# Attention edge loops of a graph network: exponentials and rescaled sum in PSUM, weighted values in a tile of their own

## What is computed

```python
def _L1_gnn_ref(node_features, edge_index, edge_relations, ...):      # 4 heads of 64
    mod_k = K[src] + 0.2 * rel_w[edge_relations][:, None, :]
    scores = jnp.einsum('ehd,ehd->eh', Q[dst], mod_k) / D ** 0.5
    ex = jnp.exp(scores - segment_max(scores, dst)[dst])
    w = ex / segment_sum(ex, dst)[dst]
    agg = segment_sum(w[:, :, None] * V[src], dst)
...
def _L2_gnn_ref(x, edge_attr, ...):                                   # 8 heads of 32
    key_j = k[src] + (edge_attr @ We + be).reshape(-1, H, C)
    alpha = softmax((q[dst] * key_j).sum(-1) / math.sqrt(C), axis=0)
    out = segment_sum(v[src] * alpha[:, :, None], dst)
```

## Time and profile before

| | us |
|---|---|
| median of three runs | 4558.12 (4556.85 to 4558.42) |
| the profiled execution, its time | 4554.94 |
| its span from first to last instruction | 4553.1 |
| layer 1, first to last L1751 | 799.7 (1832.3 to 2632.0) |
| layer 2, first to last L1751 | 844.2 (2894.8 to 3739.0) |

### The profile page before, as it was taken

The page is one execution under the profiler, slowest core; times in us unless marked ns, Lnnn a source line. Parts: engine busy times, 40 slices in busy tenths (PEclk is TensorE's granted clock), DMA queues, the critical chain, the costliest instruction groups (busy, mean ns, idle before and its releaser), DMA issues. The chain is left out here.

```text
span 4553.1 us, 52726 instructions
## 1 busy us (share of the span) xinstructions
PE 2757.1 (61%) x11454; PEld 1449.6 (32%) x11454; DVE 3258.7 (72%) x7572; ACT 720.5 (16%) x2122; POOL 3148.8 (69%) x2929
## 2 busy tenths in 40 slices
PE   4245678888885997666566757687877763000006
PEld 4145322222222885222222334344443432000004
DVE  7498358888885333788889966588888886666664
ACT  0011100000000332333323321111111112000003
POOL 0577667767664776777777757677777764777772
PEclk8555799999998998788878778778788876555558
DMA  3235346666664332655555632456666652444441
GB/s 155 41 104 157 80 139 177 177 173 172 176 173 126 57 63 58 165 160 161 160 159 163 177 67 67 134 166 168 167 167 165 169 136 60 108 108 108 108 107 41
DMA packets 408930, 594.52 MB, mean 131 GB/s; under 512 B 267146, under 2 KB 273430, under 8 KB 407806
## 3 DMA queue, kind: packets, MB, share of 16 engines
q0 software_dynamic: 185552, 519.27, 41.5%
q1 hardware_dynamic: 223278, 74.01, 6.9%
HBM read 532.97 MB, written 59.26 MB: 130 GB/s over the span
## 5 line engine op out<-in xcount | busy, mean ns | idle before, releaser
L1690 PE MATMUL edge_psX<-state,ident 128*128 128x512 f32 x720 | 480.5, 804 | 217.9 <-DMA state<-tab,edge_feat 134.3
L1106 POOL DMA_INDIRECT edge_ring<-tab,edge_rec x480 | 469.8, 979 | 146.2 <-issue 135.6
L2016 POOL DMA_INDIRECT state<-tab,edge_rec x480 | 453.8, 945 | 155.0 <-issue 145.9
L1685 PE MATMUL edge_psX<-edge_w_edge,edge_featT 64*128 64x256 f32 x1920 | 446.2, 454 | 119.6 <-DVE edge_prod L1752 117.0
L1615 POOL DMA_INDIRECT state<-tab,edge_rec x360 | 419.7, 1166 | 130.0 <-issue 108.8
L1615 POOL DMA_INDIRECT state<-tab,edge_feat x360 | 393.8, 1094 | 109.7 <-issue 100.8
L1135 PE MATMUL edge_psX<-state,ident 128*128 x720 | 380.4, 638 | 140.0 <-DVE edge_ring L1163 140.0
L1685 PEld LDWEIGHTS edge_psX<-edge_w_edge,edge_featT 64*128 64x128 f32 x1920 | 300.3, 220 | 412.6 <-issue 353.1
L2189 PE MATMUL gate_psA<-ident,gate_w_nat 128*128 128x128 f32 x8 | 2.0, 428 | 631.4 <-DMA gate_w_nat<-in_L_gnn_W_ih 631.4
L1163 DVE TENSOR_TENSOR edge_ring<-edge_psX,edge_ring 128x1024 f32<-128x1024 f32 x240 | 293.8, 1224 | 73.8 <-PE edge_psX L1142 43.8
L781 POOL DMA_INDIRECT sorted_d<-update_row_out,update_row_idx x200 | 237.7, 1189 | 91.8 <-issue 60.0
(11 more groups left out here) (447 smaller groups left out, 6513.4 us busy)
## 6 DMA issues: line engine op xcount, KB each, us to landing
sorted_d<-state SPq DMA_DIRECT2D x7, 2380.0 KB
state<-src_rows SPq DMA_DIRECT2D x25, 562.5 KB
state<-low_rows SPq DMA_DIRECT2D x25, 562.5 KB
state<-tab,edge_rec POOLq DMA_INDIRECT x840, 3.0
edge_ring<-tab,edge_rec POOLq DMA_INDIRECT x600, 3.7
update_row_out<-in_edge_attr SPq DMA_DIRECT2D x40, 156.2 KB
edge_rec<-rec_d SPq DMA_DIRECT2D x364, 8.0 KB, 2.9
state<-tab,edge_feat POOLq DMA_INDIRECT x360
```

What stands on the lines that cost most here:

```text
L1106: pool.indirect_dma_start(out=ring[:, k, s, :], out_offset=None, in_=S["tab0"][:, :], in_offset=bass.IndirectOffsetOnAxis(ap=rec[:, k, R_S ...
L1685: pe.matmul(psX[k % 2][:, s % 2, s // 2, :], featT[lo:lo + ED, k % 4, s // PAIR, :], w_edge[lo:lo + ED, :], start=(s < 2), stop=False, ski ...
L1690: last = pe.matmul(psX[k % 2][:, a, :, :], S["ident"][:, :], ring[k % RING].rearrange("p (c a) f -> p a c f", a=2)[:, a, :, 0:D], start=Fa ...
L2016: pool.indirect_dma_start(out=ring[:, k, s, :], out_offset=None, in_=S["tab3"][:, :], in_offset=bass.IndirectOffsetOnAxis(ap=rec[:, k, R_S ...
```

## The change

The tile `wgt`, two buffers in SBUF, into which ACT writes the exponentials, goes. In its place is `w`, one buffer in a PSUM bank of its own (`psW`). A second bank (`psS`) holds `so_far`, 256 numbers in each partition. The products of values and weights go to a tile `terms` in SBUF instead of back into the ring. The decayed `acc` is written to `so_far`, not in place; the first of the two remaining rows of `terms` is added to it in PSUM, and the last sum, of `so_far` and the second row, is written to `acc`. The post of s_done stands behind the halving instead of at the end of the step. The number of DVE instructions and of counted results in a step is the same.

```diff
-        wgt = ph.sb("wgt", [P, 2, ROWS, heads])
+        terms = ph.sb("terms", [P, QE, D])
...
+        psW, psS = (ph.ps(n, [P, 512]) for n in ("psW", "psS"))
+        w = psW[:, 0:ROWS * heads].rearrange("p (r h) -> p r h", h=heads)
+        so_far = psS[:, 0:D]
...
-                        act.activation(wgt[:, k % 2, :, :], cat[:, k % 2, :, :], ACT.Exp).then_inc(s_exp, 1)
+                        act.activation(w, cat[:, k % 2, :, :], ACT.Exp).then_inc(s_exp, 1)
...
+                def weigh(at):
+                    vals = ring[at][:, :, D:D2].rearrange("p s (h d) -> p s h d", h=heads)
+                    return dve.tensor_tensor(terms[:, :, :].rearrange("p s (h d) -> p s h d", h=heads), vals,
+                                             bc(w[:, 0:QE, :], 3, [P, QE, heads, hd]), ALU.mult)
+
+                def halve():
+                    return dve.tensor_tensor(terms[:, 0:2, :], terms[:, 0:2, :], terms[:, 2:4, :], ALU.add)
+
+                def decay(acc):
+                    return dve.tensor_tensor(so_far.rearrange("p (h d) -> p h d", h=heads), acc.rearrange("p (h d) -> p h d", h=heads),
+                                             bc(w[:, QE, :], 2, [P, heads, hd]), ALU.mult)
+
+                def add_half(to, i):
+                    return dve.tensor_tensor(to, so_far, terms[:, i, :], ALU.add)
...
                         hold(dve, s_exp, t * AQ + (k + 1))
                         step.put(dve.tensor_tensor(l, l, w[:, QE, :], ALU.mult))
-                        weighted = step.put(dve.tensor_tensor(vals, vals, bc(w[:, 0:QE, :], 3, [P, QE, heads, hd]), ALU.mult))
+                        weighted = step.put(weigh(at))
                         dve.wait_ge(s_xr, t * AQ + (k + 3))
                         scored = step.put(dve.tensor_reduce(score[:, 0:QE, :].rearrange("p s h -> p (s h)"),
                                                             prod[:, :, :].rearrange("p s (h d) -> p (s h) d", d=hd), AX.X, ALU.add))
                         b_next = block_of(k + 1, t) if k < AQ - 1 else None
                         step.put(dve.tensor_reduce(tot[:, :], w[:, 0:QE, :].rearrange("p r h -> p h r"), AX.X, ALU.add))
                         step.until(weighted)
-                        halved = step.put(dve.tensor_tensor(v[:, 0:2, :], v[:, 0:2, :], v[:, 2:4, :], ALU.add))
+                        halved = step.put(halve())
+                        dve.nop().then_inc(s_done[at], 1)
                         step.until(scored)
                         masked = step.put(dve.tensor_tensor(score[:, 0:QE, :], score[:, 0:QE, :], bc(mask, 2, [P, QE, heads]), ALU.add))
-                        step.put(dve.tensor_tensor(acc_h, acc_h, bc(w[:, QE, :], 2, [P, heads, hd]), ALU.mult))
+                        decayed = step.put(decay(acc))
                         step.until(masked)
                         dve.nop(nofuse=True)
                         highest = step.put(dve.tensor_reduce(m, score.rearrange("p r h -> p h r"), AX.X, ALU.max))
-                        step.until(halved)
-                        summed = step.put(dve.tensor_tensor(v[:, 0, :], v[:, 0, :], v[:, 1, :], ALU.add))
+                        step.until(decayed)
+                        summed = step.put(add_half(so_far, 0))
                         step.until(highest)
                         dve.tensor_tensor(score, score, bc(m, 1, [P, ROWS, heads]), ALU.subtract).then_inc(s_cat, 1)
                         step.put(dve.tensor_tensor(l, l, tot[:, :], ALU.add))
                         step.until(summed)
-                        step(dve.tensor_tensor(acc, acc, v[:, 0, :], ALU.add))
-                        dve.nop().then_inc(s_done[at], 1)
+                        step(add_half(acc, 1))
                         b_prev, b = b, b_next
```

More of the change, by code:

```diff
@@ L1715, in last_values @@
+                    step.put(decay(acc))
                     step(dve.tensor_reduce(tot[:, :], w[:, 0:QE, :].rearrange("p r h -> p h r"), AX.X, ALU.add))
-                    step(dve.tensor_tensor(v[:, 0:2, :], v[:, 0:2, :], v[:, 2:4, :], ALU.add))
-                    dve.tensor_tensor(acc_h, acc_h, bc(w[:, QE, :], 2, [P, heads, hd]), ALU.mult)
                     dve.tensor_tensor(l, l, tot[:, :], ALU.add)
-                    step(dve.tensor_tensor(v[:, 0, :], v[:, 0, :], v[:, 1, :], ALU.add))
```

14 lines of the change are left out of this document (5 added, 9 removed).

## The result

The changed kernel takes 4429.39 us (median of 4 runs, 4426.94 to 4430.56), the kernel before, measured beside it, 4557.49 us (4555.25 to 4558.42). The ratio is 0.9717, with an interval of 0.9706 to 0.9729: 128 us less. The forecast was 4450, with a range of 4420 to 4508. The profiled executions stand at 4430.56 and 4554.94 us, 124.4 us apart.

A forecast was written before the change was run, and what follows sets the result against it. The prediction took POOL, which issues the gathers, to bound the kernel, with DVE next. Savings of 39 us in layer 1 and 69 in layer 2 took the profiled 4554.9 to 4446.9, 4450 us as a median, range 4420 to 4508.

The forecast's parts named there:

- POOL as the bound and its reason: Both layers: POOL never waits; DVE instructions with two SBUF inputs hold its gathers and scatters, losing 104 and 100 us.
- a mean below 0.98 us: Sign of being right: L1615's gathers in both layers at a median of 946 ns and a mean under 0.98 us.
- 1.2 us a turn for the halving: POOL's remaining loss at gathers that start inside the halving, which keeps two SBUF inputs: 1.2 us a turn.
- The price of PSUM: DVE's step: the first sum's wait, the post and PSUM access together add 0.05 us a step, 6 us a layer.
- the rival with 0.07 an instruction: DVE's three 256-wide instructions each take 0.07 us more from PSUM: 4500 us; all six instructions, 4543; chance 0.09.
- the one with a product at half rate: Rival: DVE's product reads repeated PSUM weights at half rate, 1.07 us more each: +245 us, 4695; chance 0.04.
- The 512-wide row: Profile row used to price PSUM on DVE: 695 ns with 512 numbers, against 0.71 us with both inputs in SBUF.
- The post of s_done: DVE's step: moving the post out of the 0.27 us between steps gives perhaps 0.02 us back.
- The stall that goes with it: Layer 1: DVE's 5.01 us wait behind ACT's record wait moves 2 us earlier each turn, gone after the first.
- the case "it stayed": Layer 1: if the stall behind the record stayed, DVE would need 55.3 us a turn.
- Meshing in layer 2: Layer 2: POOL's 51.0 and DVE's 50.9 us turns don't mesh perfectly, adding 0.6 us a turn, 9 us.
- The sum: Layer 1 760.5 us (-39), layer 2 775.4 us (-69), together -108: 4446.9 us profiled, 4450 as a median.

The follow-up runs named there:

- weights_only_again: The changed kernel with the sums back in SBUF and the weights still in PSUM, a repeat run: 4431.2 us, 0.9728 of the kernel before.
- long runs: Follow-up runs in three of four groups, where every kernel took longer, the kernel of before by 17% (5332 to 5351 us); compared only among themselves.

## Why the prediction was right, point by point

**POOL as the bound and its reason: right.** 1.88 us became 0.95 us beside the product, and taking the weights back out of PSUM brought the long gathers back. The forecast of a mean below 0.98 us (0.975 and 0.973) holds, and so does that of 1.2 us a turn for the halving (some 13 us in 14.9 turns of layer 1 are 0.9, some 16 in layer 2 are 1.1). By the Trainium skill, "SBUF — State Buffer", section "Who interferes with whom", a `tensor_tensor` with both inputs in SBUF takes only a reading interface of the port that DVE shares with GpSimd, so that the making of descriptors is not touched (the page calls that inferred). The traces of both kernels and of the experiments disagree with that inference, with 1.88 against 0.95 us and means of 1.12 against 0.975. Which part of a gather is held they don't tell: it also reads its indices from `edge_rec` in SBUF.

**The price of PSUM: right, a little low in one place.** Of the +0.05 us a step, 0.06 was for the first sum's wait for the decay, -0.02 for the post, and next to nothing for PSUM. Measured, the product has -5 ns, the decay +8, the first sum +22, the last +1 or 2: +0.03 in durations. Neither the rival with 0.07 an instruction nor the one with a product at half rate has anything left. The 512-wide row was the better guide than the 256-wide one with another form. The wait was put too high: no run shows the 0.08 us that I took for the way of a semaphore. The first sum starts 0.03 us behind the decay's end (2105.76 after 2105.73), where it was 0.02, so its dependence cost some 0.01 and not 0.06. This and the longer sums together are the 0.03 us that weights_only_again saves. The weights in PSUM took 0.05 us off the step, which I hadn't foreseen.

**The post of s_done: mis-sized.** "Perhaps 0.02 back" was 0.11 to 0.12 us in each step. The 0.27 us of idle time before L1751 stood in the earlier trace rows, and I took it for the way of a semaphore from DVE's last sum to its next instruction. More than a third of it was the post, a `nop` that waited for that sum. Beside that the rest is small: with nothing in PSUM the step is 5.92 us, with the weights there 5.87, with the sums too 5.90. Instead of +0.05 a step there were -0.14. In floors: 731.5 us in layer 1 where 752.5 was forecast, and in layer 2, with a turn of 49.75 us, 738 where 761.4 was: 44 us below in all.

**The stall that goes with it: wrong.** "It lies earlier by 2 us more in each turn and no longer holds DVE after the first turn." It stayed in all of turns 1 to 10, at 1.6 us of DVE's time each, and 11 us in the first. The step that failed is the thought that a POOL with less work than DVE gains on it turn by turn. POOL can gain only as long as nothing holds it, and the same record that ACT waits for holds POOL too. The chain from the last scatter over SP's three loads to the record is closed by POOL itself, and 50.9 us of circle are more than DVE's 49.3. I had added up POOL's issues (47.4 us and about 1 for the halving) and left out its own wait at the turn's head, 2.2 us, which comes with the way over SP. The price of the case "it stayed" was wrong as well: not 55.3 but 50.9 us a turn, since the circle had shortened with the gathers. Layer 1 lay 28 us above its floor, where 8 were forecast. DVE's share in layer 1 (89%, "over 95%" forecast) and ACT's waits (86.9 us, "nearly gone") are the same error. POOL did sit idle for records there, as forecast, but not for want of a free slot: the wait is at the turn's head, behind the scatter. That sign came true for another reason.

**Meshing in layer 2: somewhat low.** 24 us above the floor against 5 + 9. The mean turn is 51.3 us over a floor of 49.75; POOL is full (717.7 of 720 us), with a turn of 49.8 us and 1.1 for the halving, and DVE has 91%, not 95. Since DVE turned out quicker, POOL, and not both alike, is what is left of the bound there. That is read from the busy times, not tested.

**The sum.** Errors of -44 (step) and +30 (20 in layer 1's stall, 10 in layer 2) gave a forecast that is 14 us too high in the two layers, and 4450 against 4429. The other 6 to 7 us are 2 us gained outside these spans and 4 to 5 from the step to the median: the forecast added 3.2 us to the profiled time, which lay 1.2 above the median. The total was close in part because two errors of layer 1 cancelled: -21 and +20. Its -39 against -40 looks better than it was.

## What to carry to other kernels

Where GpSimd's indirect DMAs are the bound, look for DVE instructions with two inputs in SBUF beside them, and give the longest one an input in PSUM: with the 20 or 40 weights a partition there, stalls of 147 to 164 us fell to about 30, and the sums added nothing to the gain that can be measured. A post on a semaphore at the end of a dependent step waits for that step and delays the next one; put it behind the last read of what it frees, where other work hides it. And when an engine comes off the bound, follow each wait around its whole circle before writing it off: a stall whose far end hangs on that same engine doesn't run away from it.

## What the runs showed of the hardware that was not expected

- A post behind the last instruction of a step cost 0.11 to 0.12 us (a step of 6.01 to 6.02 us with it, 5.90 without); DVE sits idle for 0.26 us ahead of the next step instead of 0.15.
- PSUM as input, or as input and output, of the 256-wide instructions costs 1 to 22 ns. The Trainium skill, "VectorE: DVE Perf Modes", section on the TRN2 errata, gives VectorE a fixed part of 58 cycles from SBUF and 120 from PSUM; the rows don't show such a difference (410 and 432 ns for the first sum, 1219 and 1214 for the product).
- In long runs the kernel of before lost 17%, with DVE waiting at "issue" for 1 to 2 us in front of its instructions, and the loss was not the same for all. With the weights in PSUM the kernels were 1.6 to 1.9% slower than the code of before beside them, while with the sums alone it was 0.2 to 0.6% and with neither nothing. Most of it lay in layer 2 (974 to 989 us, against 919 to 936 for the other versions). The undisturbed step and the gathers of these kernels are as short there as elsewhere, so it is in neither. The cause stays open. It isn't the chip alone: the one that ran the group that isn't long ran two long groups too. How the changed kernel itself does there was not measured.
